# A third position block in two fp32r parts, and layer-norm statistics by ScalarE sums in five steps

## The reference, cut to what matters

```python
x = x + _L0_xattn_ref(_layernorm(x), L0_xattn_k, bias, ctx, ctx, 8)   # causal filter along positions
x = x + _L0_ffn_ref(_layernorm(x), ...)                               # 8 experts, top 2, and a shared one
x = x + _L1_xattn_ref(_layernorm(x), ctx, seg, ...)
x = x + _L1_ffn_ref(_layernorm(x), ...)

def _layernorm(x, axis=-1, eps=1e-05):
    m = jnp.mean(x, axis=axis, keepdims=True)
    v = jnp.var(x, axis=axis, keepdims=True)
    return (x - m) / jnp.sqrt(v + eps)

# inside _L0_xattn_ref; v is the normed x, x1 = x2 = ctx; D = 256 channels are 32 heads of 8; L = 512 positions
kv = vr[:, :, :, None, :] * x2r[:, :, None, :, :]
y = irfft(rfft(kv, n=1024) * rfft(k, n=1024))[..., :512] + kv * skip
out = jnp.einsum('bhijl,bhil->bhjl', y, x1r)
```

## Time and profile before

| | us |
|---|---|
| median of 3 runs (3283.99 to 3287.28) | 3284.96 |
| profiled execution, its own time | 3289.66 |
| its span | 3287.9 |
| loop over the heads | from 25.8 to about 643 |

### The profile page before, as it was taken

The page is one execution under the profiler, slowest core; times in us unless marked ns, Lnnn a source line. Parts: engine busy times, 40 slices in busy tenths (PEclk is TensorE's granted clock), DMA queues, the critical chain, the costliest instruction groups (busy, mean ns, idle before and its releaser), DMA issues.

```text
span 3287.9 us, 51710 instructions
## 1 busy us (share of the span) xinstructions
PE 3176.7 (97%) x18581; PEld 2696.9 (82%) x18581; DVE 2174.6 (66%) x5816; ACT 1267.6 (39%) x3058; POOL 1052.6 (32%) x1114
## 2 busy tenths in 40 slices
PE   7999999999999789999999999999998999999999
PEld 4666666688899679999999999999997788888887
DVE  6888888755555477787878777777876533333332
ACT  2333333233444255555555555555554411111111
POOL 6877777535211222222222222222200111010110
PEclk9999999999999899999999999999999999999999
DMA  4544443259644432111111111111101300000000
GB/s 130 156 135 139 128 143 91 81 168 313 197 152 155 158 116 71 46 46 46 40 40 44 46 46 44 37 45 46 46 14 43 109 26 26 26 26 26 26 14 13
DMA packets 123764, 267.41 MB, mean 81 GB/s; under 512 B 17673, under 2 KB 18321, under 8 KB 123514
## 3 DMA queue, kind: packets, MB, share of 16 engines
q1 hardware_dynamic: 100122, 186.59, 18.1%
q0 software_dynamic: 23392, 77.51, 7.1%
HBM read 159.49 MB, written 104.56 MB: 80 GB/s over the span
## 4 chain that ended last, share of the span: by engine, by line
PE 78%; DVE 10%; POOL 7%; DMA 2%; ACT 1%; issue 1%; SPq 0%; POOLq 0%; DVEq 0%
PE g_PH L1039 11%; PE g_O L1062 11%; PE t_U L1505 10%; PE t_S L1457 9%; PE t_PO L1492 5%; PE t_M L1441 5%; POOL c_kf L354 3%; PE t_T L1479 3%; PE f_Y L916 3%; PE f_Y L386 2%; PE t_M L1396 2%; PE f_Y L687 2%; PE f_Y L381 2%; DVE c_R L399 2%; DVE c_z L393 2%; PE t_M L1378 2%
## 5 line engine op out<-in xcount | busy, mean ns | idle before, releaser
L1467 ACT ACTIVATE t_pr<-t_sm,t_nb 128x256 f32<-128x256 f32 x512 | 256.4, 502 | 369.2 <-DVE t_nb L1463 369.2
L1052 DVE CAST g_hh<-g_hf 128x512 fp32r<-128x512 f32 x128 | 61.8, 482 | 431.4 <-PE g_O L1062 426.8
L1411 POOL TENSOR_TENSOR t_r<-t_r 128x256 f32<-128x256 f32 x128 | 95.7, 748 | 776.0 <-DVE t_rw L1473 457.6
L354 POOL TENSOR_TENSOR c_kf<-c_vt,c_ct 128x512 f32<-128x512 f32 x256 | 296.6, 1179 | 0.2 <-PE f_Y L381 0.2
L1051 ACT ACTIVATE g_hf<-g_PH,g_b1s 128x512 f32<-128x512 f32 x128 | 88.2, 689 | 514.5 <-PE g_PH L1039 514.5
L1474 DVE TENSOR_SCALAR t_pr<-t_pr,t_rw 128x256 f32<-128x256 f32 x512 | 222.2, 434 | 18.2
L386 PE MATMUL f_Y<-c_kh,c_th 128*128 128x512 f32 x448 | 201.1, 449 | 9.2 <-ACT c_kh L361 9.2
L1039 PE MATMUL g_PH<-g_xh,g_w1h 128*128 128x512 f32 x512 | 205.3, 401 | 1.5 <-DVE g_xl L1027 1.5
L1039 PE MATMUL g_PH<-g_xh,g_w1l 128*128 128x512 f32 x512 | 202.9, 396 | 0.0
L1039 PE MATMUL g_PH<-g_xl,g_w1h 128*128 128x512 f32 x512 | 202.6, 396 | 0.0
L1062 PE MATMUL g_O<-g_w2h,g_hh 128*128 128x512 f32 x512 | 202.4, 395 | 0.0
(11 more groups left out here) (355 smaller groups left out, 9695.1 us busy)
## 6 DMA issues: line engine op xcount, KB each, us to landing
xs<-c_zero SPq DMA_DIRECT2D x71, 256.0 KB, 5.2
f_xg<-xs SPq DMA_DIRECT2D x71, 256.0 KB, 2.8
ys<-f_yt POOLq DMA_DIRECT2D x71, 256.0 KB, 2.4
c_tr<-kpad SPq DMA_DIRECT2D x60, 256.0 KB, 4.8
f_xg<-xn SPq DMA_DIRECT2D x40, 256.0 KB
c_xt<-x SPq DMA_DIRECT2D x32, 256.0 KB, 3.5
c_cr<-ctx SPq DMA_DIRECT2D x32, 256.0 KB, 3.9
c_ct<-ctxh SPq DMA_DIRECT2D x32, 256.0 KB, 4.3
```

Source lines behind the costliest of these rows:

```text
L354: T["kv", h] = T["kv1", n] = p.do("gpsimd", lambda e: e.tensor_tensor(o, iv, ic, ALU.mult), g("vt", h), g("ct", h), g("kl", n - 8), g("kh" ...
L1467: T["ex", x] = p.do("scalar", lambda e, t=t, k4=k4: e.activation(pr[:, N % 2, t, :], sm[:, k4, :], ACT.Exp, bias=nb[:, k4, 0:1], scale=-1. ...
```

## The change

Four things are done together, all in the front phase.

1. Position block 2 is split like blocks 0 and 1: in `conv`, its one fp32 matmul becomes three fp32r ones (in `lb` 2 and 3 of both halves, four times a head). `kh` and `kl` get a third block; the low part is made by VectorE for `u` 0 and by GpSimd for `u` 1. `t0` is needed for one block of 128 only.
2. The statistics of both norms leave `bn_stats`. For the first norm ScalarE sums `xt` (`total`), VectorE scales the sum to minus the mean (`centre`), ScalarE sums the squares of `xt` minus the mean (`squares`), VectorE scales and adds eps (`stats`), GpSimd takes the power (`power`). For the second norm the sum comes out of `finish`, whose addition is now one VectorE instruction that also gives its row sums, and the mean stands right behind it; `squares0`, `stats0`, `power0` follow.
3. These pieces stand one step apart: `total`, `centre`, `squares`, `stats`, `power` of head `h+2` in steps 3 to 7, and the mean, `squares0`, `stats0`, `power0`, `shift0` of head `h-1` in steps 3 to 7.
4. The rest is moved: `shift(h+1)` from step 7 of the head before to step 0, `norm` from 0 to 1, `weigh` from 0 to 2, `load` from 2 to 0, `norm0` from 6 to step 0 of the next head, `turn0` from 7 to 1, and `logit` from behind `conv` of step 1 to ahead of `conv` of step 2.

```diff
+    def total(h):
+        a = p.do("scalar", lambda e: e.activation(ju[:, :], xt[:, h % 4, :], ACT.Copy, accum_out=S_[:, 0:1]), g("x", h), g("xn", h - 2), U.get("ju"))
+    def centre(h):
+        T["mean", h] = p.do("vector", lambda e: e.tensor_scalar(S_[:, 1:2], S_[:, 0:1], -1.0 / 512.0, None, ALU.mult), a, g("xn", h - 2))
+    def squares(h):
+        T["sq", h] = U["ju"] = p.do("scalar", lambda e: e.activation(ju[:, :], xt[:, h % 4, :], ACT.Square, bias=S_[:, 1:2], accum_out=S_[:, 2:3]),
+                                    T["mean", h], g("x", h), U["ju"])
...
-        if mb > 1:
+        if mb > 2:
             return
         T["kh", n] = p.do("scalar", lambda e: e.activation(kh[:, v, mb, :], kf[:, v, mb, :], ACT.Copy), g("kv1", n), g("mmu", 2 * h + u - 2))
-        if low or mb % 2:
+        if low or mb == 1 or mb == 2 and u:
             lows(h, u, mb)
...
-            if mb > 1:
+            if mb > 2:
                 last = p.do("tensor", lambda e, c=c, mb=mb: e.matmul(Y[y % 4][:, :], t0[:, s, c], kf[:, v, mb, :], start=False, stop=mb == lb),
...
-        T["out2", h] = U["PR",] = p.do("vector", lambda e: e.tensor_tensor(xt[:, h % 4, :], sk[:, s, :], PR[:, :], ALU.add), g("pr", h), g("sk", h))
+        T["out2", h] = U["PR",] = p.do("vector", lambda e: e.tensor_tensor_reduce(
+            out=xt[:, h % 4, :], in0=PR[:, :], in1=sk[:, s, :], scale=1.0, scalar=0.0, op0=ALU.add, op1=ALU.add, accum_out=S_[:, 0:1]),
+            g("pr", h), g("sk", h), gu("xb", h - 2))
+        U["mean", h] = p.do("vector", lambda e: e.tensor_scalar(S_[:, 1:2], S_[:, 0:1], -1.0 / 512.0, None, ALU.mult), T["out2", h], gu("xb", h - 2))
...
+                if at == 3:
+                    if more:
+                        turn(h + 1)
+                    if soon:
+                        total(h + 2)
+                if at == 4:
+                    if more:
+                        filt(h + 1)
+                    if soon:
+                        centre(h + 2)
+                    if h:
+                        squares0(h - 1)
+                if at == 5:
+                    if soon:
+                        squares(h + 2)
+                    if h:
+                        stats0(h - 1)
...
```

More of the change, by code:

```diff
@@ L367, in lows @@
         n = (2 * h + u) * 4 + mb
-        eng = "gpsimd" if mb % 2 else "vector"
+        eng = "gpsimd" if mb == 1 or mb == 2 and u else "vector"
         T["kl", n] = p.do(eng, lambda e: e.tensor_tensor(kl[:, v, mb, :], kf[:, v, mb, :], f32(kh[:, v, mb, :]), ALU.subtract),
@@ L700, in front_phase @@
     load(1)
+    total(0)
+    centre(0)
+    squares(0)
     stats(0)
+    power(0)
     filt(0)
@@ L709, in front_phase @@
     residual(0)
+    total(1)
+    centre(1)
+    squares(1)
     stats(1)
-    shift(1)
+    power(1)
     split_filters()
@@ L736, in front_phase @@
[L736 to L739, removed]
+                at = 4 * u + lb
+                soon = h + 2 < n_heads
+                if at == 0:
+                    if h > 1:
+                        norm0(h - 2)
+                    if soon:
+                        load(h + 2)
+                    if more:
+                        shift(h + 1)
+                if at == 1:
+                    if more:
+                        norm(h + 1)
+                    if h > 1:
+                        turn0(h - 2)
@@ new lines, in front_phase @@
+                if at == 5:
+                    if soon:
+                        squares(h + 2)
+                    if h:
+                        stats0(h - 1)
+                if at == 6:
+                    if more:
+                        filt_lo(h + 1)
+                    if soon:
+                        stats(h + 2)
+                    if h:
+                        power0(h - 1)
+                if at == 7:
+                    if soon:
+                        power(h + 2)
+                    if h:
+                        shift0(h - 1)
@@ L744, in front_phase @@
                     parts(*units[n], low=False)
-                conv(h, u, lb, units[n] if n < len(units) and lb == 0 else None)
+                conv(h, u, lb, units[n] if n < len(units) and (lb == 0 or lb == 2 and not units[n][1]) else None)
                 if u == 0 and lb == 3 and h:
@@ L751, in front_phase @@
                     residual(h + 1)
-                if u == 0 and lb == 1:
+                if at == 1:
                     shared_weights()
-                    if h > 1:
-                        logit(h - 2)
-                if u == 0 and lb == 3 and h > 1:
+                if at == 4 and h > 1:
                     best(h - 2)
-                if u == 1 and lb == 0 and h > 8 and h % 8 == 1:
+                if at == 5 and h > 8 and h % 8 == 1:
                     choose(h // 8 - 1)
-                if h and u == 1:
-                    (stats0, shift0, norm0, turn0)[lb](h - 1)
                 if not more and u == 0:
@@ L795, in more @@
             pend.append((fetch(src), to, c, ("w1",) if to is w1f else ("w2",)))
-    events = {0: [lambda: finish(last), lambda: logit(last - 1), lambda: stats0(last), lambda: shift0(last), lambda: norm0(last)], 1: [lambda: best(last - 1)],
-              3: [lambda: turn0(last)], 4: [lambda: logit(last)], 5: [lambda: best(last), lambda: choose(3)], 7: [ranks], 8: [offsets],
+    events = {0: [lambda: norm0(last - 1), lambda: finish(last), lambda: squares0(last), lambda: turn0(last - 1), lambda: stats0(last), lambda: power0(last)],
+              1: [lambda: logit(last - 1), lambda: shift0(last), lambda: norm0(last)], 2: [lambda: best(last - 1)], 3: [lambda: turn0(last)], 4: [lambda: logit(last)], 5: [lambda: best(last), lambda: choose(3)], 7: [ranks], 8: [offsets],
               9: [places, by_head], 10: [experts], 11: [biases]}
```

72 lines of the change are left out of this document (46 added, 26 removed).

## The result

The changed kernel takes 3327.99 us (median of 4 runs, 3324.53 to 3329.78), the kernel before 3285.56 beside it: a ratio of 1.0129, 95% interval 1.0117 to 1.0141. The profiled execution took 3326.52 with a span of 3324.7; before it was 3289.66 and 3287.9. The split and the five steps made the kernel slower by 42 us in the median, 37 in the profiled pair.

The account below looks back on a forecast made before the run. A loop of waits through four engines, 0.43 us longer than TensorE's work, sets the pace. Heads +25.9, last distance +1.4 and start -0.9 make +26.4, giving 3311 us; range 3293 to 3341, the forecast case's own 3294 to 3326.

Parts of the forecast that it names:

- the forecast's own signs of being wrong: In the profile after: a head distance of 17.9 with no stall there, or matmuls with the lower clock inside the loop.
- The loop: Waits through VectorE, ScalarE, GpSimd and TensorE: head 19.95 us against 18.95, with stalls of 0.9 at `turn0`, 1.15 at `logit`.
- The unknown prices: Fused sum in `finish` taken as 0.68 us (bounds 0.6 and 1.3), ScalarE's squares as 0.70 (bounds 0.57 and 0.81).
- GpSimd's contention: GpSimd's step-6 product, disturbed by VectorE's new low part, was to take 1.45 us; undisturbed, the head would be 0.4 shorter.
- TensorE's own work: Per head, four fp32 matmuls become three fp32r each, 0.62 us less: from 18.52 to 17.90.
- The shared weights: Heads that also split shared weights: their 3.1 us in all is covered by GpSimd's 2.7 idle per head.
- The start: Twelve steps ahead of 53.48: three halves, each 0.31 us cheaper, and no such stall, -0.9.
- Rival 1: New TensorE stalls lower its clock, 1.85 us each in a third to all of 30 heads: 3330 to 3367; chance 0.20.
- `choose`: Three heads with `choose`, now one step later, left at the old price of 6.5 us for the three.
- The end of the loop: Too mixed to work out, put at 0, give or take 3 us; the last distance separately at +1.4.
- TensorE-bound: Rival 2: neither `xT` nor `xb` late, TensorE's own work sets a head of 17.90 us, total 3249; chance 0.12.
- The even case: Rival 3: loop 0.8 to 1.1 us shorter than forecast, head near 18.95, total 3281 to 3289; chance 0.06.

Follow-up runs that it names:

- the copy on the loop: Changed kernel with one more ScalarE copy of 128 x 512 right behind `squares0`: 3345.42 us; off the loop, behind `total` in step 3: 3315.95 us.
- the fastest run: Changed kernel with squares behind `kh`, `turn0` in step 2, `logit` in step 3, `turn` behind `conv` of step 3: 3246.4 us, ratio 0.989.
- e7_choose_later: Changed kernel with `choose` moved from step 5 of a head to step 1 of the next: 3311.56 us, ratio 1.0089.
- the layout with `choose` later: Kernel with squares behind `kh` and `turn0`, `logit`, `turn` late, with `choose` also moved to step 1 of the next head: 3258.41 us, ratio 0.9914.

## Why the prediction was right

The time of 3327.99 lies in the range of 3293 to 3341, 17 above the predicted 3311 and 2 above the forecast's own range, which ended at 3326. The mechanism and the length of the loop are as forecast. Even so, one of the forecast's own signs of being wrong came true: matmuls show the lower clock inside the loop. And that the total came so near is in part luck, for terms of both signs were off.

**The loop.** It runs as drawn. Counted from the end of `conv` in step 3, at 408.79, forecast and trace: `squares0` at 2.45 and 2.45; GpSimd's low part at 5.05 and 5.09; first power at 6.75 and 6.77; last product at its end 11.53, the `kh` behind it at 11.61; `turn0` at 10.55 and 10.51; `logit` at 13.55 and 13.48. The head was 19.95 and is 19.94. (Two slips of its working are small: 13.55 and 6.42 make 19.97, and the two transposes named for the old head stand 18.93 apart, where 18.95 is the mean.) The experiments confirm it from both sides: the copy on the loop is paid in full, off it not at all, and the squares out of the way give 1.03.

**The unknown prices.** The fused sum took 0.68 as taken, and its accumulator 0.08. `squares` took 0.70 from start to the next start and `squares0` 0.72, with 0.70 taken; the accumulator of `squares0` is read from 411.87 to 412.05, and the next instruction starts at 411.96. GpSimd's contention hit another instruction than the forecast said. Line 377, then line 368, of the changed kernel, as in the earlier trace rows:

```profile
L377 POOL TENSOR_TENSOR c_kf<-c_vt,c_ct x256: 1054/1071/1532, 23.3 to 672.2; 128x512 f32<-128x512 f32 x128
```
```profile
L368 POOL TENSOR_TENSOR c_sk<-c_sk,c_xt x32: 1262/1740/1747, 18.1 to 665.7; 128x512 f32<-128x512 f32 x32
```

The product of step 6 was undisturbed (1.03 in the chain, 1.45 forecast) and `residual` paid (1.69, 1.24 forecast). Their sum, 2.72 against 2.69, came out right by two errors that cancel. Who pays goes by who is first. GpSimd's product of step 6 and its `residual`, with VectorE's low part of step 6 between them, in this head; then `residual` in the run with the squares behind `kh`, where VectorE's stands at 407.51:

```profile
416.07 1.07 POOL L377 TENSOR_TENSOR c_kf<-c_vt,c_ct 128x512 f32<-128x512 f32 x1
416.78 0.90 DVE L392 TENSOR_TENSOR c_kl<-c_kf,c_kh 128x512 fp32r<-128x512 f32 x1
417.10 1.73 POOL L368 TENSOR_TENSOR c_sk<-c_sk,c_xt 128x512 f32<-128x512 f32 x1
```
```profile
407.43 1.29 POOL L368 TENSOR_TENSOR c_sk<-c_sk,c_xt 128x512 f32<-128x512 f32 x1
```

Here the product is 0.71 ahead of VectorE's low part, and it is the low part that is 0.22 longer (0.90 for 0.68). The low part starts 0.3 ahead of `residual`, and `residual` is 0.45 longer. There it starts 0.08 behind, `residual` takes its 1.29, and the low part 1.1 more. The Trainium skill states it so ("SBUF — State Buffer", section "Who interferes with whom"): issue order decides which one blocks. By that rule, the trace agrees. The forecast had the right order in its own times, the product at 7.3 and the low part at 8.0, and let the product pay all the same.

**TensorE's own work** was put at 17.90 and is 17.68 where nothing waits. Printed waits are 0.85 and 0.92, 1.77 in all, where 2.05 stood in the forecast, with the same distance. `turn0` and `logit` themselves are longer behind a wait (0.66 and 1.06 against 0.60 and 0.99 in the fastest run), so a wait costs more than the idle time printed in front of it.

**The shared weights** are covered as forecast: their heads are 19.94 too. **The start** gave 0.66, forecast 0.9.

**The terms that were mis-sized.** Three, of both signs:

- The clock. Rival 1 held in part: 7 of 29 heads, a quarter, 1.57 each, 11.0 us, and the first head 1.6 for its longer wait. The rival was priced at a third to all of the heads with 1.85 each, as a case of its own; the forecast's sum held none of it.
- `choose`. It was left "at the old price of 6.5 for the three", and is 14.5. The prediction named that it stands one step later, but not what is queued behind it there: the statistics of steps 6 and 7, now on the loop.
- The end of the loop. It was put at 0, give or take 3; with the last distances it gave 8.6 back, where +1.4 stood in the sum. Of these, 3.3 lie in the last two distances (33.55 before, 30.30 after) and 2.7 in the 40 us behind them. Windows over the last of the loop and the 20 us behind it, before and after (from the last `finish` transposes at 646.18 and 688.39):

```profile
646.00:666.00 20.00, 17.33 (x117) 15.95 (x117) 7.54 (x24) 7.06 (x15) 0.55 (x1) 0.91 0.24 79
```
```profile
688.00:708.00 20.00, 19.26 (x138) 17.13 (x137) 9.33 (x29) 9.57 (x19) 0.57 (x2) 1.00 0.29 93
```

Before, the wait of 1.88 and the lower clock of the earlier trace rows were followed by a wait of 2.67 at 652.20 and a second fall. After, the same places have 1.22 and 0.24, and the clock stays full in these 20 us. That fits the 6.0 of these two parts, but no run varied the loop's end by itself. The last 2.6 belong to code that the change doesn't touch: the second phase (which the earlier trace rows calls the third) took 1357.5 before and 1354.9 after, from the first of its sums (line 1463 before, 1539 after) to the last, and between 1352.9 and 1358.1 in the thirteen traces of this case. Nothing of the change answers for them.

In the sum: 26.4 forecast, plus 12.6 (clock and first head), plus 8.0 (`choose`), less 10.0 (end), and 0.2 less for roundings and the start, is the 36.8 of the trace. So 20.6 more than forecast on one side stand against 10.0 less on the other, and 2.6 of these have nothing to do with the change.

**The other rivals.** TensorE-bound (3249) was false for this kernel, and what it would take is shown by the run of 3246.4: no piece of the loop was missing, but its reader on TensorE had to stand later. The even case would have needed a head near 18.95; the place of the squares alone makes it (18.91, 3285.89).

## What to carry to other kernels

When several engines form a loop, price a change by where each instruction stands in its queue, and by when the loop's result is read: here the same instructions took 3328, 3286 or 3246 us by order alone. Shortening the engine at the end of such a loop gave nothing until its reads stood later than the loop's result. Of an instruction that is moved, look at what is queued behind it at its new place on every engine that it uses, anew in each layout.

## What the hardware showed that was not expected

- Equal waits at equal places in equal heads gave the lower clock (1.2 instead of 2.4 GHz, granted 0.54) in seven heads and not in the others; longer waits (1.50 and 0.91) gave it in none, and a single wait of 3.40 or 3.41, at the `choose` heads of the run with the squares behind `kh`, in one of three. Filling the waits with matmuls took it away. A fall cost 1.57 us.
- Tiny VectorE instructions with two operands in SBUF can wait for a whole GpSimd instruction. The addition of `choose` (128x64, line 565, 0.23 at 559.38 of the run e7_choose_later) took 1.10 at 226.53 of the changed kernel, beside a product of GpSimd from 226.48 on:

```profile
226.48 1.07 POOL L377 TENSOR_TENSOR c_kf<-c_vt,c_ct 128x512 f32<-128x512 f32 x1
```

  In the layout with `choose` later, the 128x8 subtraction of line 553 took 0.99 from 214.47 beside a product from 214.37 for 1.06, and 0.18 in the changed kernel with no GpSimd instruction beside it. So a chain of ten such pieces has no fixed price; no run took the GpSimd work away, so this rests on rows alone.
